# A two-layer graph convolution on one core: rows sent by kind, tile 1 decoded like later tiles, VectorE's constants in its waits, other counts of idle products, and the last position turned

## The chip, the cores and the metric

The kernel runs on one core of a Trainium2 chip. The metric is the device time of one execution in microseconds (us), the median of several runs. Engines are named TensorE (PE in the rows; PEld is its weight load), VectorE (DVE), ScalarE (ACT), GpSimd (POOL) and SyncE (SP). SPq, ACTq and POOLq are the DMA issues of an engine.

## The reference

There are 6250 nodes with 64 features and 200000 edges, sorted by destination. Cut to what matters:

```
deg_out = clip(segment_sum(1, src), 1);  deg_in = clip(segment_sum(1, dst), 1)
norm    = rsqrt(deg_out[src] * deg_in[dst])
conv(x, W1, W2):
    msg = (x[src] @ W1 + (x[src] * x[dst]) @ W2) * norm
    return x @ W1 + segment_sum(msg, dst)
h = relu(layernorm(x));  h = relu(conv(h, W1_1, W2_1));  h = conv(h, W1_2, W2_2)
out = x + h
```

With S = sum over a node's edges of x[src] / sqrt(deg_out), a layer is x @ W1 + (S @ W1 + (S * x) @ W2) / sqrt(deg_in). The kernel computes that form.

## The kernel before

Nodes are laid out in 49 blocks of 128 (node 128 b + 4 r + s sits in partition 32 s + r of block b). The kernel makes a dense count matrix of the edges and multiplies with it, in four stages.

**Opening.** SyncE loads dst (L395, L396), then the last entries of each row (`prev_i`, L398, behind a memset by GpSimd) and four weight matrices (L402). VectorE makes its constants (L609 to L620; the last ones, `mask`, `of_v` and `select`, are what the edge weights are computed with), casts the samples of dst, `last` and `prev` (L625 to L628), and chooses rows (`choose_rows`, L631, L632). TensorE multiplies the choice with the samples (the windows, L910: one product for tile 0, six for tiles 1 to 6). VectorE counts, per tile, where each row begins (`find_begin`, L640 to L645), and GpSimd fetches the edges of a row of that tile with indirect DMAs (`fetch`, L480: src and dst apart). There are seven tiles of seven blocks; `p_rows` is what becomes keys, `rows` (three kinds: place, place x q, place x q x q) what becomes weights. Tile 0 and tile 1 are decoded by VectorE (`decode_early`, L652 to L670; tile 1 after block 2), the later tiles by GpSimd in five steps beside the units (`decode`, L493, by `DECODE`) with VectorE's `weigh` (L672) between them. For tiles 0 and 1 TensorE turns `p_rows` (`turn`, L914) and ScalarE copies it to `keys` (`save_keys`, L1056); for the later ones SyncE writes eight DMAs to a table (`turn_keys`, L414) and issues one transposing DMA. The rows go to the `stack`: for tile 0, the first two blocks straight from `rows`, six DMAs, five by SyncE (L408) and one by ScalarE (L1093), all behind `rows_ready`; all others through a table (L409 to L413, L437 to L443). After tile 1's rows SyncE loads x (`load_x`). TensorE issues products that nobody reads (`keep_running`, L897: 36, 28 and 90 of them) where it would stand still.

**Units.** There are 98 units, two per block. Before the products of a unit (`products`, L938: 24 products of 98 columns into a `slab`), TensorE computes pairs of edge weights (`weigh_hots`, L923: 2 products of 392 columns per pair, three pairs for two units), ScalarE saves each pair (`save_weights`, L1069), and after the unit it packs the slab to `words` (`save_words`, L1080). VectorE makes the low one-hots of a block (`low_hots`, L683, a ring of three). `pairs_beside(u)` says which pairs TensorE and ScalarE do with unit u: they are four pairs ahead of what the unit reads from unit 0 on. VectorE's statistics of x lie beside blocks 9 to 27 (`STATS_BESIDE`, three per block), parts of `unpack` beside later ones.

**Turn to layer 0.** After unit 97 VectorE sums the degrees; ScalarE takes the root; VectorE scales h by pieces (`scaled_piece`), ScalarE applies relu to each piece (the high part, L1113), VectorE takes the low part (`low_piece`). TensorE multiplies positions 0, 1 and 2 together as the pieces come (L1017).

**Positions.** 98 positions, 49 per layer: 49 products of 128 or 129 columns each (L1039), the tile of counts stationary, the parts of h moving. For a position that is done, ScalarE and VectorE form S (`save_sums`, `sums`), GpSimd the product with h, TensorE turns the pair (`turn_pair`, L979, fp32), ScalarE saves it (`save_t`), TensorE multiplies it with the weights (`weigh`, L991) and VectorE adds it into g1 or `x_sb` (`finish`, L829). In layer 1 this is done inside the next position, behind product 26 (`EARLY`) and product 43 (`LATE`). In the last position TensorE sums three totals behind product 23 (L1045 to L1048), one of which is the check that no packed count is full (L886, L887). The end of the last position is then done alone (L1051, L1052), SyncE stores the result (L446 to L450, four DMAs for each of five stretches), and the flag decides whether the general path is run (it is not, here).

Queues: each engine takes its instructions in the order written. Nothing is planned at run time; semaphores hold each where it reads what another writes.

## Time and profile before

| | us |
|---|---|
| median of 3 runs | 507.52 (507.25 to 509.15) |
| the profiled execution | 506.1 |
| its span | 504.4 |
| TensorE busy | 484.3 |
| VectorE busy | 422.3 |
| ScalarE busy | 249.7 |
| GpSimd busy | 139.1 |
| opening, to the first weighing | 0 to 22.3 |
| units | 24.5 to 185.8 |
| turn to layer 0 | 185.8 to 199.4 |
| positions 3 to 97 | 199.4 to 497.7 |
| end | 497.7 to 504.4 |

The span begins and ends with the engines' first and last instruction; the time of an execution also holds what lies around it, 1.7 us here. Rows with an instruction begin with its start from the span's start, then its duration.

### The profile page before, as it was taken

How to read it: one execution, taken by the hardware profiler on the slowest of the kernel's cores; microseconds unless marked ns; L12 is line 12 of the kernel's file. 1: busy time of each engine (PE TensorE's matmuls, PEld its weight loads, DVE VectorE, ACT ScalarE, POOL GpSimd, SP SyncE). 2: the span in 40 equal slices, each digit the busy share in tenths (PEclk: the TensorE clock that was granted, in tenths of full speed). 3: DMA queues.
4: the chain of work that ended last, by engine and by line, in shares of the span. 5: the costliest groups of instructions: out<-in, count | busy, mean ns of one | idle time of the engine just before them, and what ended most of it. 6: DMA issues, size and time to landing. Idle time of an engine off the chain costs nothing.

```text
span 504.4 us, 19900 instructions
## 1 busy us (share of the span) xinstructions
PE 484.3 (96%) x8018; PEld 458.6 (91%) x8018; DVE 422.3 (84%) x1092; ACT 249.7 (50%) x706; POOL 139.1 (28%) x376
## 2 busy tenths in 40 slices
PE   5889999999999979999999999999999999999994
PEld 5768888888888869999999999999999999999993
DVE  6999999999999957877777777777988888888883
ACT  1299999999999964433333333332111111111110
POOL 3412434334346301433333333332111111111110
PEclk9999999999999998999999999999999999999998
DMA  3258313021202000000000000000000200010000
GB/s 69 79 102 97 66 28 83 23 73 33 58 15 54 3 1 3 4 1 3 3 3 2 4 3 3 4 1 3 4 3 2 45 3 1 3 44 1 14 18 18
DMA packets 24791, 12.32 MB, mean 24 GB/s; under 512 B 21024, under 2 KB 23376, under 8 KB 24701
## 3 DMA queue, kind: packets, MB, share of 16 engines
q1 hardware_dynamic: 23997, 9.04, 9.2%
q0 software_dynamic: 672, 2.01, 1.4%
q8 instruction: 64, 1.05, 0.9%
q14 instruction: 26, 0.21, 0.1%
q10 hardware_dynamic: 32, 0.01, 0.0%
HBM read 6.21 MB, written 4.05 MB: 20 GB/s over the span
## 4 chain that ended last, share of the span: by engine, by line
PE 88%; ACT 4%; DVE 4%; DMA 2%; issue 1%; SPq 0%; DVEq 0%; ACTq 0%
PE diff L1039 35%; PE slab L951 19%; PE iota_bank L1039 17%; PE diff L933 9%; ACT hots L1076 3%; PE diff L1010 2%; PE diff L1017 1%; PE slab L988 1%; DMA los<-in_dst_dram 1%; PE turn_t L988 1%; PE diff L1006 1%; ACT words L1084 1%; PE iota_bank L1017 1%; PE slab L1039 1%; DMA mixed<-rows 1%
## 5 line engine op out<-in xcount | busy, mean ns | idle before, releaser
L694 DVE TENSOR_TENSOR los<-mixed,iota_bank 128x5120 bf16<-128x5120 bf16 x49 | 137.5, 2809 | 5.2 <-PE slab L951 4.6
L951 PEld LDWEIGHTS slab<-hots,los 128*128 128x128 bf16 x2352 | 119.5, 98 | 13.6 <-ACT hots L1076 0.6
L951 PE MATMUL slab<-hots,los 128*128 128x98 fp8e5 x2352 | 125.4, 209 | 0.2 <-ACT hots L1076 0.2
L1076 ACT ACTIVATE hots<-diff 128x784 f16<-128x784 f32 x147 | 118.4, 848 | 6.3 <-PE diff L933 6.2
L1039 PE MATMUL diff<-late,mixed 128*128 128x128 f16 x1616 | 104.4, 219 | 0.0
L1039 PEld LDWEIGHTS diff<-late,mixed 128*128 128x128 fp8e4 x1616 | 98.7, 99 | 0.4
L1039 PE MATMUL diff<-los,mixed 128*128 128x129 f16 x1470 | 95.6, 220 | 0.0
L576 POOL TENSOR_TENSOR work<-work,h 128x64 f32<-128x64 f32 x98 | 31.5, 321 | 228.2 <-DVE work L811 228.2
L1039 PEld LDWEIGHTS diff<-los,mixed 128*128 128x128 fp8e4 x1470 | 89.3, 98 | 0.3
L933 PE MATMUL diff<-select,mixed 80*128 80x392 f16 x294 | 65.2, 329 | 3.2 <-ACT hots L1076 2.4
L740 DVE TENSOR_SCALAR mixed<-words 128x400 int32<-128x400 int32 x192 | 61.1, 358 | 0.0
L1084 ACT ACTIVATE words<-slab 128x441 uint16<-128x441 f32 x98 | 59.9, 611 | 2.2 <-PE slab L951 1.2
L1039 PE MATMUL iota_bank<-late,tile 128*128 128x128 f16 x784 | 51.5, 219 | 0.0
L1039 PE MATMUL iota_bank<-los,tile 128*128 128x129 f16 x735 | 49.0, 220 | 0.0
L1039 PEld LDWEIGHTS iota_bank<-late,tile 128*128 128x128 fp8e4 x784 | 48.0, 99 | 0.2
L1039 PEld LDWEIGHTS iota_bank<-los,tile 128*128 128x128 fp8e4 x735 | 45.0, 98 | 0.2
L487 POOL TENSOR_TENSOR hist<-hist,words 128x49 int32<-128x49 int32 x48 | 15.5, 324 | 104.9 <-ACT words L1084 81.1
L818 DVE SCALAR_TENSOR_TENSOR work<-h,stats,work 128x64 f32<-128x64 f32 x98 | 39.5, 403 | 4.5
L933 PEld LDWEIGHTS diff<-select,mixed 80*128 80x128 f16 x294 | 23.4, 98 | 12.2 <-ACT hots L1076 4.6
L740 DVE TENSOR_SCALAR tile<-words 128x400 int32<-128x400 int32 x96 | 30.6, 357 | 0.0
L1147 ACT ACTIVATE work<-diff,unscale 128x64 f32<-128x64 f32 x33 | 10.3, 313 | 38.1 <-PE diff L1039 37.1
L881 DVE TENSOR_TENSOR largest<-largest,words 128x900 uint16<-128x900 uint16 x47 | 29.0, 616 | 0.1
(177 smaller groups left out, 535.1 us busy)
## 6 DMA issues: line engine op xcount, KB each, us to landing
x_sb<-in_x_dram SPq DMA_DIRECT2D x4, 384.0 KB
rows_table<-rows SPq DMA_DIRECT2D x6, 252.0 KB, 2.5
mixed<-rows_table SPq DMA_DIRECT2D x18, 84.0 KB, 2.9
out_dram<-x_sb SPq DMA_DIRECT2D x8, 128.0 KB
los<-in_dst_dram SPq DMA_DIRECT2D x1, 750.0 KB
p_table<-p_rows_sb SPq DMA_DIRECT2D x20, 28.0 KB
p_table<-p_rows_sb SPq DMA_DIRECT2D x20, 7.0 KB
out_dram<-x_sb SPq DMA_DIRECT2D x4, 80.0 KB
```

The costliest lines, as they stand in the source:

```text
L487: nc.gpsimd.tensor_tensor(out=hist[:], in0=hist[:], in1=words[:, b, 0:Q - 1, WORDS // 2:WORDS // 2 + 2].bitcast(I32)[:, :, 0], op=ALU.add) ...
L576: nc.gpsimd.tensor_tensor(out=pair[a][:, 1], in0=s_sum[a], in1=h[:, b], op=ALU.mult).then_inc(product_ready, 1)
L694: nc.vector.tensor_tensor(out=los[:, b % LOS_RING].rearrange("e s (v t) -> e s v t", t=2), in0=key, in1=val, op=ALU.is_equal).then_inc(los ...
L740: ins = nc.vector.tensor_scalar(to, packed, 2 * s, 0x03030303, ALU.logical_shift_right, ALU.bitwise_and)
L818: nc.vector.scalar_tensor_tensor(pair[a][:, 0], h[:, b], root[:, b:b + 1], s_sum[a], ALU.mult, ALU.add).then_inc(pair_ready, 1)
L881: nc.vector.tensor_tensor(out=largest[:], in0=largest[:] if b > 1 else flat_words[:, 0:Q * SLOTS], in1=words[:, b].rearrange("p q s -> p ( ...
L933: ins = nc.tensor.matmul(diff[m % 2][:, bank, 0:HALF], stack[0:80, t % 2, j, k * 128:(k + 1) * 128], select[0:80, i * HALF:(i + 1) * HALF] ...
L951: ins = nc.tensor.matmul(to, los[:, u // 2 % LOS_RING, u % 2 * ULOWS + low], pairs, start=(step == 0), stop=(step == USTEPS - 1), skip_gro ...
L1039: ins = nc.tensor.matmul(bank(n)[:, 0:width], tiles[home(n)][:, q], parts[:, q, 0:width], start=(q == 0), stop=(q == BLOCKS - 1))
L1076: nc.scalar.activation(bass.AP(to.tensor, to.offset, [to.ap[0], [step, 2], [STEPS * BLOCKS, 8], [1, BLOCKS]]), diff[m % 2][:, :, 0:HALF].r ...
L1084: nc.scalar.activation(words[:, u // 2, 0:Q - 1, 9 * (u % 2):9 * (u % 2) + 9], bass.AP(mine.tensor, mine.offset + first, [mine.ap[0], [1, ...
L1147: nc.scalar.activation(s_hi[a], bank(n)[:, 0:D], ACT.Copy, scale=unscale).then_inc(hi_saved, 1)
```

## The change

- **Rows by kind.** Tile 0's rows are decoded in the same order, but each kind counts a semaphore of its own (`early_rows_ready` 1 and 2, then `rows_ready`). For the first two blocks SyncE sends kind 0 of both after the first, ScalarE kind 1 of both after the second, and after the third each sends one DMA of kind 2.
- **Tile 1 like later tiles.** GpSimd decodes it (steps 0 to 2 before unit 0, steps 3 and 4 at units 1 and 2), VectorE's `weigh(1)` stands after block 2, and its keys take SyncE's eight DMAs and the transposing DMA; TensorE's second `turn` and ScalarE's second `save_keys` go. x is loaded behind all that, and its statistics lie beside blocks 11 to 30.
- **Constants in waits.** VectorE's `mask` to `select` move between the begin of tile 0 and the windows of the others. The offset and the cast of prev come before the wait for dst. ScalarE casts the samples and issues the DMA of `prev_i`, of which GpSimd sets only row 0. The weights' DMAs wait for dst. Tiles 1 to 5 are counted with one comparison and one reduction.
- **Order of pairs.** TensorE and ScalarE have two pairs ahead at units 0 and 1, three at 2 and 3, four from unit 4 on.
- **Idle products.** 24, 28 and 76 in the opening; 34 more after unit 97 and 12 more ahead of the third round of pieces.
- **VectorE's own first pieces.** It applies relu to the first piece itself and takes the low parts of the first two pieces before it scales the third.
- **Last position turned.** Its 49 products have the parts stationary and the tile moving, so that S comes out turned, twice (S on partitions 0 to 63 and again, as high and low part, on 64 to 127). h of the last block is turned in position 95 and its product with W1 (`own_ps`) is added to `x_sb` in position 96. VectorE then scales S, and multiplies it with h turned; two fp32 products with weights stored twice give the rest. The sum of totals moves behind product 45. Two of the last four stores are issued by ScalarE.

```
```diff
+    DECODE.update({1: (1, 3), 2: (1, 4)})
+    WEIGH_BESIDE = {2: 1, **{u0 // 2 + 5: t for t, u0 in BEGIN.items()}}
...
-    STATS_BESIDE = [b for b in range(9, 34) if b not in WEIGH_BESIDE][:17]
+    STATS_BESIDE = [b for b in range(11, 34) if b not in WEIGH_BESIDE][:17]
...
+    def made(u):
+
+        return min(pairs_of(u) + 2 + min(u // 2, 2), UNITS * STEPS // 2)
+
     def pairs_beside(u):
 
-        first = 3 * (u // 2) + 4
-        return [m for m in ((first, first + 1) if u % 2 == 0 else (first + 2,)) if m < UNITS * STEPS // 2]
+        return range(made(u - 1) if u else 0, made(u))
...
-            sp.wait_ge(prev_set, 1)
-            sp.dma_start(prev_i[1:SROWS], bass.AP(dst.tensor, dst.offset + ROWLEN - GRAIN,
-                                                  [[ROWLEN, SROWS - 1], [1, GRAIN]])).then_inc(prev_in, 16)
+            sp.wait_ge(dst_in, 32)
...
             sp.wait_ge(stack_zeroed, 1)
+            sp.wait_ge(early_rows_ready, 1)
+            for j in range(2):
+                sp.dma_start(stack[0:16, 0, j], rows[16 * j:16 * j + 16, 0]).then_inc(first_in[j], 16)
             sp.wait_ge(rows_ready, 1)
-            for j in range(2):
-                for k in range(3):
-                    if (j, k) != (0, 1):
-                        sp.dma_start(stack[32 * k:32 * k + 16, 0, j], rows[16 * j:16 * j + 16, k]).then_inc(first_in[j], 16)
+            sp.dma_start(stack[64:80, 0, 0], rows[0:16, 2]).then_inc(first_in[0], 16)
...
+            def save_p(t):
                 sp.wait_ge(p_saved, t + 1)
-                if t > 2:
-                    sp.wait_ge(keys_in, 16 * (t - 2))
...
+            def turn_keys(t):
+                sp.wait_ge(p_out, 16 * 8 * t)
...
+            def save_rows(t):
+                sp.wait_ge(rows_ready, t + 1)
+                sp.wait_ge(stack_in, 48 * t)
+                sp.dma_start(rtab, rows[:]).then_inc(rows_out, 16)
+
             for t in range(1, TILES):
-                if t >= 2:
-                    turn_keys(t)
-                sp.wait_ge(rows_ready, t + 1)
+                save_p(t)
                 if t == 1:
-                    sp.wait_ge(rest_in, 48)
+                    save_rows(t)
...
             for b0, b1 in STORES:
                 sp.wait_ge(y_ready, b1)
-                for s in range(4):
+                for s in range(4 if b1 < BLOCKS else 2):
...
+            for step in range(3):
+                decode(1, step)
...
+            v(nc.vector.tensor_scalar(offset[:], group0[:], -1.0, 1.0, ALU.mult, ALU.add))
+            dve.wait_ge(prev_set, 1)
             dve.wait_ge(prev_in, 16)
             v(nc.vector.tensor_copy(prev[:], prev_i[:, GRAIN - 1:GRAIN]))
+            dve.wait_ge(dst_in, 32)
+            v(nc.vector.tensor_copy(last[:], dst_i[:, ROWLEN - 1:ROWLEN]))
...
+            def find_begins():
+                dve.wait_ge(window_ready, 2)
+                v(nc.vector.tensor_tensor(out=junk[:, 1:6], in0=windows[1][:, :, 0:SAMPLES],
+                                          in1=group0[:, 1:6].unsqueeze(2).to_broadcast([ROWS, 5, SAMPLES]), op=ALU.is_lt))
+                v(nc.vector.tensor_reduce(out=before[:, 1:6], in_=junk[:, 1:6], axis=AX.X, op=ALU.add))
+                count_before(6, windows[2][:, 0])
+                add_windows(1, 6, windows[1])
+                add_windows(6, TILES, windows[2])
+                bound_begin(1, TILES)
...
+                v(nc.vector.scalar_tensor_tensor(rows[:, 0].bitcast(U16), place, 8 * 2048.0, place, ALU.is_le, ALU.mult))
+                nc.vector.tensor_tensor(out=shared, in0=shared, in1=own, op=ALU.mult).then_inc(early_rows_ready, 1)
+                dve.wait_ge(early_rows_ready, 1)
+                nc.vector.scalar_tensor_tensor(rows[:, 1], q_i, -float(MID), rows[:, 0], ALU.add,
+                                               ALU.mult).then_inc(early_rows_ready, 1)
+                dve.wait_ge(early_rows_ready, 2)
+                nc.vector.scalar_tensor_tensor(rows[:, 2], q_i, -float(MID), rows[:, 1], ALU.add,
+                                               ALU.mult).then_inc(rows_ready, 1)
...
+            scaled_piece(1)
+            qs = slice(*PIECES[0])
+            dve.wait_ge(scaled_ready, 1)
+            nc.vector.tensor_scalar(parts0[:, qs, 0:D], scaled[:, qs], 0.0, None, ALU.max).then_inc(first_hi0_ready, 1)
+            low_piece(0)
+            low_piece(1)
+            scaled_piece(2)
+            for i in range(3, len(PIECES)):
...
+                    dve.wait_ge(own_ready, 1)
+                    v(nc.vector.tensor_tensor(out=x_sb[:, BLOCKS - 1], in0=x_sb[:, BLOCKS - 1], in1=own_ps, op=ALU.add))
                     dve.wait_ge(largest_taken, BLOCKS - 1)
-                    v(nc.vector.tensor_scalar(largest[:], largest[:], FULL, None, ALU.is_ge))
-                    nc.vector.tensor_reduce(out=totals[:, 2:3], in_=largest[:], axis=AX.X,
-                                            op=ALU.max).then_inc(totals_ready, 1)
+                    v(nc.vector.tensor_reduce(out=totals[:, 2:3], in_=largest[:], axis=AX.X, op=ALU.max))
+                    nc.vector.tensor_scalar(totals[:, 2:3], totals[:, 2:3], FULL, None, ALU.is_ge).then_inc(totals_ready, 1)
                 if n == POSITIONS - 1:
-                    dve.wait_ge(totals_summed, 1)
+                    dve.wait_ge(acc_ready, n + 1)
+                    nc.vector.tensor_scalar(s_t, bank(n)[:, 0:128], unscale1[:, 0:1], None,
+                                            ALU.mult).then_inc(last_ready, 1)
+                    dve.wait_ge(h_t_saved, 1)
+                    nc.vector.scalar_tensor_tensor(product_t, bank(n)[:, 0:128], unscale1[:, 0:1], h_t,
+                                                   ALU.mult, ALU.mult).then_inc(last_ready, 1)
+            dve.wait_ge(totals_summed, 1)
...
-            keep_running(36)
+            keep_running(24)
...
-            turn(0)
-            keep_running(90)
+            turn()
+            keep_running(76)
...
+            keep_running(34)
...
+                if i == 2:
+                    keep_running(12)
...
+                    if n == POSITIONS - 1:
+                        ins = nc.tensor.matmul(bank(n)[:, 0:128], parts1[:, q, 0:2 * D], tiles[home(n)][:, q],
+                                               start=(q == 0), stop=(q == BLOCKS - 1))
+                    else:
+                        ins = nc.tensor.matmul(bank(n)[:, 0:width], tiles[home(n)][:, q], parts[:, q, 0:width],
+                                               start=(q == 0), stop=(q == BLOCKS - 1))
+                    if n == POSITIONS - 3 and q == EARLY - 16:
+                        pe.wait_ge(z_used, BLOCKS)
+                        for half in range(2):
+                            turned_h = nc.tensor.matmul(h_turn_ps[half * D:(half + 1) * D], h[:, BLOCKS - 1], ident[:],
+                                                        start=True, stop=True)
+                        turned_h.then_inc(h_turned, 1)
+                    if n == POSITIONS - 2 and q == EARLY + 8:
+                        pe.wait_ge(h_t_saved, 1)
+                        nc.tensor.matmul(own_ps, h_t[0:D], wt[0:D, 1], start=True, stop=True).then_inc(own_ready, 1)
                     if q in turns:
                         turn_pair(turns[q])
                     if q in weighs:
                         weigh(weighs[q])
-                    if n == POSITIONS - 1 and q == EARLY - 3:
+                    if n == POSITIONS - 1 and q == LATE + 2:
...
-            turn_pair(POSITIONS - 1)
-            weigh(POSITIONS - 1)
+            n = POSITIONS - 1
+            pe.wait_ge(w_in, 128)
+            pe.wait_ge(y_ready, n - 1 - BLOCKS)
+            pe.wait_ge(last_ready, 1)
+            nc.tensor.matmul(turn_z[n % 2][:, 0:D], s_t, wt_twice[:, 0], start=True, stop=False)
+            pe.wait_ge(last_ready, 2)
+            nc.tensor.matmul(turn_z[n % 2][:, 0:D], product_t, wt_twice[:, 1], start=False, stop=True).then_inc(z_ready, 1)
...
+            act.wait_ge(dst_in, 32)
+            nc.scalar.activation(samples[:, 0:SAMPLES], dst_i[:, GRAIN - 1:ROWLEN:GRAIN], ACT.Copy).then_inc(samples_ready, 1)
+            save_keys()
...
+            act.wait_ge(early_rows_ready, 2)
+            for j in range(2):
+                act.dma_start(stack[32:48, 0, j], rows[16 * j:16 * j + 16, 1]).then_inc(first_in[j], 16)
             act.wait_ge(rows_ready, 1)
-            act.dma_start(stack[32:48, 0, 0], rows[0:16, 1]).then_inc(first_in[0], 16)
-            for m in range(4):
-                save_weights(m)
+            act.dma_start(stack[64:80, 0, 1], rows[16:32, 2]).then_inc(first_in[1], 16)
...
+                if n == POSITIONS - 2:
+                    act.wait_ge(h_turned, 1)
+                    nc.scalar.activation(h_t, h_turn_ps, ACT.Copy).then_inc(h_t_saved, 1)
...
+            act.wait_ge(y_ready, BLOCKS)
+            for s in range(2, 4):
+                part, n = node_rows(out, s, BLOCKS - 1, BLOCKS)
+                act.dma_start(part, x_sb[32 * s:32 * s + n, BLOCKS - 1:BLOCKS]).then_inc(y_out, 16)
```

## Rows read from the trace of the kernel before

**Rows 1.** The page: busy time of TensorE; the chain, by engine.
```profile
PE 484.3 (96%) x8018; PEld 458.6 (91%) x8018; DVE 422.3 (84%) x1092; ACT 249.7 (50%) x706; POOL 139.1 (28%) x376
...
PE 88%; ACT 4%; DVE 4%; DMA 2%; issue 1%; SPq 0%; DVEq 0%; ACTq 0%
```

**Rows 2.** Timeline of TensorE to 40 us: start, duration, instruction, idle before.
```profile
3.37 4.02 PE L900 MATMUL diff<-identb 128*128 128x128 bf16 x36 [3.37 <-POOL identb L474]
...
16.37 5.19 PE L900 MATMUL diff<-identb 128*128 128x128 bf16 x90
22.31 0.82 PE L933 MATMUL diff<-select,mixed 80*128 80x392 f16 x4 [0.76 <-DMA mixed<-rows]
...
37.10 0.51 PE L933 MATMUL diff<-select,mixed 80*128 80x392 f16 x2 [0.64 <-ACT hots L1076]
```

**Rows 3.** Timeline of VectorE to 40 us.
```profile
7.29 0.24 DVE L625 CAST los<-los 125x100 f32<-125x100 int32 x1 [0.23 <-DMA los<-in_dst_dram]
...
9.81 0.16 DVE L650 TENSOR_SCALAR offset<-group 112x7 f32<-112x7 f32 x1
...
12.55 0.32 DVE L640 TENSOR_SCALAR_CACHE_REDUCE los<-diff,group 112x100 bf16<-112x100 f32 x1 [1.83 <-PE diff L910]
...
15.21 0.35 DVE L658 TENSOR_SCALAR work<-late 112x384 int32<-112x384 int32 x1
```

**Rows 4.** Timeline of GpSimd to 40 us.
```profile
11.69 1.17 POOL L480 DMA_INDIRECT late<-in_src_dram,begin_i  x1 [7.52 <-DVE begin_i L645]
...
16.81 1.26 POOL L480 DMA_INDIRECT late<-in_dst_dram,begin_i  x1 [0.31 <-issue]
```

**Rows 5.** All instructions of line 408: durations in ns, first and last start.
```profile
L408 SPq DMA_DIRECT2D mixed<-rows x5: 589/589/606, 18.9 to 21.4; - x5
...
DMA to landing us min/median/max: 1.8/2.0/2.6
```

**Rows 6.** Timeline of ScalarE to 40 us.
```profile
26.12 2.28 ACT L1076 ACTIVATE hots<-diff 128x784 f16<-128x784 f32 x3 [1.00 <-PE diff L933]
...
34.69 0.62 ACT L1060 ACTIVATE mixed<-turn_t 128x224 bf16<-128x224 f32 x2
```

**Rows 7.** Timeline of SyncE's queue, 36 to 72 us.
```profile
35.67 6.88 SPq L393 DMA_DIRECT2D x_sb<-in_x_dram  x5
50.68 0.98 SPq L421 DMA_DIRECT2D p_table<-p_rows_sb  x1
...
63.83 1.26 SPq L442 DMA_DIRECT2D mixed<-rows_table  x3
```

**Rows 8.** Windows of 1 us: five engines' busy time, granted clock, DMA.
```profile
191.00:192.00 1.00, 1.00 (x13) 1.00 (x11) 1.00 (x3) 0.51 (x2) 0.00 (x0) 0.50 0.00 0
```

**Rows 9.** Timeline of TensorE, 176 to 216 us.
```profile
188.44 0.51 PE L1017 MATMUL diff<-los,late 128*128 128x129 f16 x6 [2.64 <-DVE los L790]
...
190.29 1.70 PE L1017 MATMUL diff<-los,late 128*128 128x129 f16 x14 [0.26 <-DVE los L790]
...
194.11 0.98 PE L1017 MATMUL diff<-los,late 128*128 128x129 f16 x14
...
199.41 1.39 PE L1039 MATMUL slab<-los,mixed 128*128 128x129 f16 x21
```

**Rows 10.** Timeline of VectorE, 474 to 505 us.
```profile
494.50 1.09 DVE L887 TENSOR_REDUCE totals<-largest 128x1 f32<-128x900 uint16 x1
...
500.20 0.28 DVE L839 SCALAR_TENSOR_TENSOR x_sb<-diff,stats,x_sb 128x64 f32<-128x64 f32 x1 [0.69 <-PE diff L1010]
```

**Rows 11.** Timeline of TensorE, 474 to 505 us.
```profile
495.64 0.19 PE L1047 MATMUL slab<-totals,ones 128*1 128x3 f32 x2 [1.32 <-DVE totals L887]
...
497.03 0.39 PE L1010 MATMUL diff<-wt,work 128*128 128x64 f32 x2
497.25 0.45 PE L1039 MATMUL diff<-late,mixed 128*128 128x128 f16 x5
```

**Rows 12.** Line 450 (stores) from 497 us, durations in ns.
```profile
L450 SPq DMA_DIRECT2D out_dram<-x_sb x8: 293/343/446, 497.8 to 501.6; - x8
```

198 lines of the change are left out of this document (95 added, 103 removed).

## The prediction

> **What bounds the kernel now.** I read the page first: busy shares and the chain by engine [rows 1]. The reader is to see that TensorE is busy 96% of the span and holds 88% of the chain. Every other engine matters only where TensorE waits. So I next looked for TensorE's idle time in the timeline, and found it in three places: the opening, up to unit 6 [rows 2 to 7]; the turn from the histogram to layer 0 [rows 8, 9]; and the last position [rows 10 to 12]. Between them it never stands for as much as half a microsecond at a time, and the change moves only VectorE's statistics there, two blocks later. The sum below is therefore three local sums, made against the profiled execution: 506.1 us, of which 504.4 is span.
>
> **Opening, up to the first weighing.** Before, the first weighing starts at 22.31 and is released by a DMA of rows [rows 2]. Backwards from there:
> - VectorE's casts of samples and prev (pitches of 0.15 and 0.19) go from between dst's landing and the choice of rows: the first to ScalarE (cast beside `last` and `later`, 0.5 us of cover), the second in front of the wait. The offset (0.20) goes ahead too. So begin 0 is found 0.54 earlier, and that is what the first fetch waits for.
> - In the wait for the windows (1.83 idle [rows 3]) VectorE now builds `mask` to `select`, 5.00 to 7.06 before, 2.1 us. It then comes to the windows at 12.3, and TensorE has them at about 12.2: no loss, no cover left.
> - Five counts of 0.37 pitch become one comparison of 500 elements and one reduction. No row shows them. Nearest is a reduction of 900 elements in 1.09 us [rows 10]: by its share 0.6 for each of the two, 1.2 for both, between 0.9 and 1.8. Begin 1 to 6 is then found at 14.6 and not at 15.3.
> - Decoding tile 0 starts at 15.21 before, behind those counts [rows 3]. It now starts when the counts end or the first fetch lands, if that is later. The fetch is issued at 11.69 before [rows 4], 0.54 earlier after, and landed in at most 3.5 us: by 14.7. I take 0.6 earlier; bounds 0.2 and 0.8.
> - SyncE issues its five row DMAs one behind another from 18.9, 0.59 to 0.61 each [rows 5]; the second, begun at 19.5, holds up unit 0. Now kinds 0 and 1 go while kinds 1 and 2 are still computed (0.6 each), half of them by ScalarE, idle then. At `rows_ready` only one issue is left ahead of unit 0. That is worth one issue, 0.6, plus up to 0.3 of spread in landing (1.8 to 2.6 [rows 5]).
> Together 1.4 us earlier, weighing at 20.9; bounds 0.6 and 1.9. The dst DMA no longer shares the engines with the weights' four DMAs; I count 0 to 0.3 for it, inside the bounds. Prev's DMA goes ahead of ScalarE's table load (1.28), whose result is wanted only at 16.6; the smaller memset and the merged semaphores cost and bring nothing, since their engines wait there.
>
> The selection work now lies beside GpSimd's first fetch. The first fetch takes 1.17 us beside an idle VectorE and one beside its decoding 1.26 [rows 4], so at most 0.3 is lost. [...]
>
> **Idle products.** 36 become 24, 90 become 76. The spacing tells the clock: 36 in 4.02 us is 112 ns each, 90 in 5.19 is 58 [rows 2]; the granted column says 1.00 throughout this stretch and is of no use here. So the 1.2 GHz level holds until after the second batch (28), the 2.4 GHz level from 16.4. With 76 x 58 ns from 15.7 the third batch ends at 20.1, before 20.9. If the clock rises 2 us later it ends at 21.1 and costs 0.2.
>
> **Units 0 to 6.** Tile 1 loses TensorE's turn (0.15) and ScalarE's four copies, 1.05 us from 34.69 to 35.74. TensorE's wait of 0.64 at 37.10 is for a weight save queued behind them [rows 2, 6]. That is 0.8. The new order puts unit 1 at two pairs less, so it begins over 1 us earlier. Unit 4 has its pairs as late as before, since ScalarE must by then have saved as many. I take 0.7; bounds 0.15 (the turn alone) and 1.7 (ScalarE's 1.00 idle ahead of 26.12 as well). VectorE gives back 2 us (four of decode_early's seven operations go), so it is not the next bound. It has 5.2 us of idle over all 49 blocks.
>
> **What is queued behind.** SyncE now carries tile 1's keys: 8 issues of 0.85, the transposition 2.23, and only then x [rows 7]. From 26.9 that is 38.8 for x and 47.3 for its last issue, where before it ended at 42.6. First, keys of tile 1 are wanted by VectorE at 41.3 (block 7) and land at 39.3. Second, x is wanted from block 11, 58 us. Third, tile 2's save is free to start at 47.9. Its rows are issued at 63.83 and land at 66.9, where the weighing for unit 28 starts at 68.0: 1 us of slack, and x ends just before. I count none of it and keep 1 us for the range. GpSimd's decoding of tile 1 (0.51, 0.51, 0.58) fits from 18.5 to 21.2, five microseconds before VectorE's `weigh`.
>
> **The turn to layer 0.** TensorE is idle 2.64 us before the first piece at 188.44. The granted clock is 0.50 from 190.4 to 193.7, and 14 products take 1.70 us where 14 later take 0.98 [rows 8, 9]. The 34 idle products (2.0 us at 58 ns) fill the wait, end at 187.7, and delay nothing; 12 more fill the wait for piece 2 (0.7 us). With the high clock: 18 products of the third round from 190.35, then five rounds of 21 and one of 7, all at 58 ns, so 190.35 + 1.05 + 5 x 1.22 + 0.41 = 197.9. VectorE's pieces arrive each 1.07 and stay ahead. Before it is 199.41: 1.5 us. VectorE's own first pieces make piece 1 ready 0.5 earlier, which lands in the wait for piece 2 (ready 0.1 later). Bounds: 0 if the clock falls all the same, 1.9.
>
> **The tail.** Added: in positions 95 and 96 three fp32 products, of 128, 128 and 64 columns. An fp32 product of 64 columns holds TensorE 0.22 (two instructions from 497.03, the next product at 497.25 [rows 11]), so 0.22, 0.22 and 0.22, up to 1.1 if 128 columns cost twice; 0.7. Removed:
> - TensorE's wait of 1.32 for the totals (reduction 494.50 to 495.59 [rows 10, 11]). Its product moves behind product 45, which runs at 496.4 with the 0.7 above; the totals come at 496.3, as VectorE shifts too. The whole wait goes, 1.45 with the restart behind it; the slack is 0.1.
> - From the last product's end to the last `x_sb`: 497.70, ScalarE 497.74, VectorE 498.14 and 498.46, TensorE 498.96, ScalarE 499.32, TensorE 499.65, VectorE 500.20 [rows 10], 2.5 us. After: two VectorE operations on 128 columns (0.3, 0.35), one fp32 product (0.44) and three hand-overs, 1.3; VectorE comes 0.1 late from position 96's own sum.
> The last `x_sb`: 0.7 - 1.45 - 1.1, or 1.9 earlier. Then two stores of four go to ScalarE: they are issued from 500.5 to 501.9 at 0.34 each [rows 12], so 0.6. The maximum is taken before the comparison (0.15 on one column for 0.38 on 900), which pays for the sum of own products (0.2). The second copy of the weights is loaded before layer 0, with DMA idle. The flag's four small operations (0.7) now stand behind the last `x_sb`, under the stores' landing. Tail: 2.5; bounds 1.2 and 3.5.
>
> **Sum.** 1.4 + 0.7 + 1.5 + 2.5 = 6.1 us off 506.1, which is 500.0 for a profiled execution. The median of the runs lies 1.4 above the profiled one, 507.5, so **501.4**.
>
> **Rivals.**
> 1. As summed: 72%.
> 2. TensorE's clock falls at the turn to layer 0 after all, or begin and rows gain little because a fetch or a landing takes the place: 1.5 or 1.0 of the sum is gone, in the worst case both, so 503 to 504. For it: even now the clock falls 2 us after TensorE has resumed, so what precedes decides. Against it: the wait is filled. 15%.
> 3. A queue takes over: keys of tile 1 or rows of tile 2 come late behind x on SyncE. Each stalls TensorE once, 1 to 3 us, so 502.5 to 504.5. For it: 1 us of slack. Against it: the save starts at its old distance to TensorE. 8%.
> 4. Slower than before: the clock at the opening. TensorE does 26 idle products less, and stands 2.2 us ahead of the first window, where it stood 1.2. If its clock were still low in the third batch, 76 x 112 ns would end at 24.2, 3.3 late, and each microsecond of units at 1.2 GHz costs half of itself. To lose all 6.1, it must stay low until about 30. Rising at 33, 509. For it: 64 products and 7 windows had not raised it before. Against it: the last batch follows without more idle than now. 3%.
> 5. An edit does not do what it says, as where the last position's weights (fp16, changed per product) cannot hide their load: 49 x 50 ns, 2.4 us, so 503.8. Unit products with 16-bit weights come each 47 ns (24 in 1.12 us), which speaks against it. 2%.
>
> A measurement of this kernel tells 0.5%, 2.5 us, from no change, so faster means below 505.0. Case 1 is faster, and most of 2, 3 and 5; about 9 in 100 of all lose enough to stay within it, and case 4 is the slower side: faster 0.88, same 0.09, slower 0.03. The range for 8 in 10 goes from 499.3 (sum 8.2) to 505.0 (2.5), taking in most of cases 2 and 3. All lower bounds together would be 2.0 and all upper ones 9.0, neither of them likely.
>
> **What would show it.** First weighing at 20.9 and unit 6 at 35.3; x's last issue before 48; no granted clock of 0.50 around 190; layer 0's fourth position 3.6 earlier than 199.4; no TensorE wait in the last position; 1.3 us from its last product to the last `x_sb`. The sum is wrong if the third batch of idle products is spaced 112 ns, or if units wait for a DMA near 45 or 66.

## The result and the profile after

The changed kernel takes 504.0 us (median of 4 runs, 503.6 to 505.4) beside 508.0 for the kernel before, measured with it: a ratio of 0.9926 (95% interval 0.9904 to 0.9948), 4.0 us faster. In two later groups of runs the same two kernels gave 501.8 for 506.2 (0.9925, 0.9895 to 0.9954) and 501.5 for 505.6 (0.9909, 0.9885 to 0.9932). So the gain is 4.0 to 4.4 us where 6.1 were forecast. The first profile after is of the 505.4 us run, the slowest of its four; its span is 503.6.

The page after, busy times and chain [rows 1]: TensorE's share of the chain is now 91% (88 before), and ScalarE's and VectorE's have halved, from 4% to 2% each.
```profile
PE 485.2 (96%) x8042; PEld 457.8 (91%) x8042; DVE 422.7 (84%) x1081; ACT 248.5 (49%) x701; POOL 142.1 (28%) x380
...
PE 91%; DVE 2%; DMA 2%; ACT 2%; issue 1%; SPq 0%; POOL 0%; DVEq 0%; ACTq 0%; POOLq 0%
```
TensorE's timeline in the opening, after [rows 2]. The third batch of idle products is spaced 58 ns (76 in 4.41), and the first weighing starts at 20.86, as forecast. But unit 0 (24 products from 23.35) takes 2.13 us, where 24 took 1.29 before: the granted clock falls to 0.50 at 23.4, for 3.4 us. This is called the low clock below (1.2 GHz; 1.00 is 2.4).
```profile
15.43 4.41 PE L955 MATMUL diff<-identb 128*128 128x128 bf16 x76
20.86 0.82 PE L986 MATMUL diff<-select,mixed 80*128 80x392 f16 x4 [1.02 <-DMA mixed<-rows]
...
23.35 2.13 PE L1004 MATMUL slab<-hots,los 128*128 128x98 fp8e5 x24
25.28 0.85 PE L986 MATMUL diff<-select,mixed 80*128 80x392 f16 x2
25.92 1.69 PE L1004 MATMUL slab<-hots,los 128*128 128x98 fp8e5 x24
```
VectorE after [rows 3]: the unshown pair, one comparison and one reduction, took 0.66 and 0.67 (forecast 0.6 each), and decoding starts at 14.27, 0.94 earlier.
```profile
12.03 0.66 DVE L672 TENSOR_TENSOR los<-diff,group 112x500 bf16<-112x500 f32 x1
12.73 0.67 DVE L674 TENSOR_REDUCE before<-los 112x5 f32<-112x500 bf16 x1
...
14.27 0.35 DVE L688 TENSOR_SCALAR work<-late 112x384 int32<-112x384 int32 x1
```
GpSimd after [rows 4]. The fetch beside `select` took 1.17 us again, as beside an idle VectorE, so that overlap cost nothing. The last row is one to keep in mind: tile 2's sources are now fetched at 22.06.
```profile
11.10 1.17 POOL L502 DMA_INDIRECT late<-in_src_dram,begin_i  x1 [6.93 <-DVE begin_i L661]
...
22.06 1.00 POOL L502 DMA_INDIRECT late<-in_src_dram,begin_i  x1 [0.28 <-issue]
```
SyncE's queue after, around x [rows 7]: tile 1's keys are turned at 35.53, x goes from 38.38 to 47.3, tile 2's rows at 63.17. No unit waited for a DMA, so rival 3 did not come.
```profile
35.53 1.24 SPq L439 DMA_TRANSPOSE mixed<-p_table  x1
37.01 1.32 SPq L460 DMA_DIRECT2D mixed<-rows_table  x3
38.38 8.88 SPq L405 DMA_DIRECT2D x_sb<-in_x_dram  x8
...
63.17 1.27 SPq L460 DMA_DIRECT2D mixed<-rows_table  x3
```
The turn to layer 0 after, TensorE [rows 9]. The 14 products at 190.80 are those of the first two rounds, those at 192.85 begin the third. They take 0.98 where they took 1.70: there is no low clock.
```profile
187.79 2.06 PE L955 MATMUL diff<-identb 128*128 128x128 bf16 x34
190.80 0.97 PE L1064 MATMUL diff<-los,late 128*128 128x129 f16 x14 [0.95 <-DVE los L831]
...
192.85 0.98 PE L1064 MATMUL diff<-los,late 128*128 128x129 f16 x14 [0.23 <-DVE los L831]
...
200.44 1.39 PE L1090 MATMUL slab<-los,mixed 128*128 128x129 f16 x21
```
The tail after, VectorE and TensorE [rows 10, 11]: no wait for the totals, last product ends at 498.54, last `x_sb` starts at 499.74.
```profile
498.58 0.35 DVE L940 TENSOR_SCALAR mixed<-diff,unscale 128x128 f32<-128x128 f32 x1 [0.22 <-PE diff L1087]
498.85 0.34 DVE L943 SCALAR_TENSOR_TENSOR mixed<-diff,unscale,mixed 128x128 f32<-128x128 f32 x1
499.74 0.28 DVE L887 SCALAR_TENSOR_TENSOR x_sb<-diff,stats,x_sb 128x64 f32<-128x64 f32 x1 [0.56 <-PE diff L1117]
```
```profile
488.60 0.44 PE L1095 MATMUL slab<-ident,h 128*64 128x128 f32 x4
...
498.07 0.19 PE L1107 MATMUL slab<-totals,ones 128*1 128x3 f32 x2
498.20 0.34 PE L1087 MATMUL diff<-mixed,late 128*128 128x128 fp8e4 x3
499.07 0.41 PE L1115 MATMUL diff<-mixed 128*128 128x64 f32 x2 [0.53 <-DVE mixed L940]
```
The stores: SyncE [rows 12] and ScalarE. The last is issued 1.0 us earlier than before, but the program ends only 0.8 earlier.
```profile
L472 SPq DMA_DIRECT2D out_dram<-x_sb x6: 313/400/446, 498.4 to 500.6; - x6
```

### The profile page after: what moved, and what is told of

Its sections match the earlier page's. It is cut to its first block, busy times and chain, and to the rows that moved or that the text cites. A ratio compares the mean times of both kernels' runs of the same rounds, so it can differ in the third digit from the quotient of the medians.

```text
span 503.6 us, 19945 instructions
## 1 busy us (share of the span) xinstructions
PE 485.2 (96%) x8042; PEld 457.8 (91%) x8042; DVE 422.7 (84%) x1081; ACT 248.5 (49%) x701; POOL 142.1 (28%) x380
## 4 chain that ended last, share of the span: by engine, by line
PE 91%; DVE 2%; DMA 2%; ACT 2%; issue 1%; SPq 0%; POOL 0%; DVEq 0%; ACTq 0%; POOLq 0%
PE diff L1090 34%; PE slab L1004 21%; PE iota_bank L1090 17%; PE diff L986 10%; PE diff L1055 2%; ACT hots L1141 1%; PE turn_t L1033 1%; DMA los<-in_dst_dram 1%; PE diff L1051 1%; PE slab L1033 1%; PE diff L1064 1%; PE slab L1090 1%; PE diff L1087 1%; DMA late<-in_dst_dram,begin_i 1%; PE iota_bank L1064 1%
## 5 line engine op out<-in xcount | busy, mean ns | idle before, releaser
L1004 PEld LDWEIGHTS slab<-hots,los 128*128 128x128 bf16 x2352 | 120.8, 98 | 13.3 <-issue 0.3
L1004 PE MATMUL slab<-hots,los 128*128 128x98 fp8e5 x2352 | 126.6, 209 | 0.0
L1090 PE MATMUL diff<-late,mixed 128*128 128x128 f16 x1567 | 101.3, 219 | 0.0
L1090 PEld LDWEIGHTS diff<-late,mixed 128*128 128x128 fp8e4 x1567 | 95.8, 98 | 0.5
L1090 PE MATMUL diff<-los,mixed 128*128 128x129 f16 x1470 | 95.7, 220 | 0.0
L1090 PEld LDWEIGHTS diff<-los,mixed 128*128 128x128 fp8e4 x1470 | 89.3, 98 | 0.3
L986 PE MATMUL diff<-select,mixed 80*128 80x392 f16 x294 | 66.6, 330 | 5.0 <-ACT hots L1141 3.9
L1090 PE MATMUL iota_bank<-late,tile 128*128 128x128 f16 x784 | 51.7, 219 | 0.0
L1090 PE MATMUL iota_bank<-los,tile 128*128 128x129 f16 x735 | 49.0, 220 | 0.0
L1090 PEld LDWEIGHTS iota_bank<-late,tile 128*128 128x128 fp8e4 x784 | 48.0, 98 | 0.4 <-issue 0.2
L1090 PEld LDWEIGHTS iota_bank<-los,tile 128*128 128x128 fp8e4 x735 | 45.1, 98 | 0.2
L986 PEld LDWEIGHTS diff<-select,mixed 80*128 80x128 f16 x294 | 22.9, 98 | 15.6 <-ACT hots L1141 8.8
```

The costliest lines, as they stand in the source:

```text
L986: ins = nc.tensor.matmul(diff[m % 2][:, bank, 0:HALF], stack[0:80, t % 2, j, k * 128:(k + 1) * 128], select[0:80, i * HALF:(i + 1) * HALF] ...
L1004: ins = nc.tensor.matmul(to, los[:, u // 2 % LOS_RING, u % 2 * ULOWS + low], pairs, start=(step == 0), stop=(step == USTEPS - 1), skip_gro ...
L1090: ins = nc.tensor.matmul(bank(n)[:, 0:width], tiles[home(n)][:, q], parts[:, q, 0:width], start=(q == 0), stop=(q == BLOCKS - 1))
```

## One span cut into stages, for every kernel run

Since each profile is of one execution, and these differ by 5 us for one and the same kernel, I cut every span at the same marks of TensorE: the first weighing, unit 6, the last unit product, position 3, position 93. A mark is the start of the weight load, which lies up to 0.2 us ahead of the product itself. The columns add up to the span (us), but for rounding.

| profile of | 1st weighing | to unit 6 | to last unit product | to pos. 3 | to pos. 93 | to end | span |
|---|---|---|---|---|---|---|---|
| before, 1st | 22.3 | 15.0 | 148.3 | 13.8 | 280.9 | 24.1 | 504.4 |
| before_again | 22.3 | 15.3 | 150.5 | 12.8 | 280.9 | 24.1 | 506.0 |
| before_fetch_late | 21.6 | 15.7 | 148.7 | 13.8 | 280.9 | 24.1 | 504.8 |
| after, 1st | 20.8 | 16.6 | 150.3 | 12.7 | 280.9 | 22.3 | 503.6 |
| after_again | 20.9 | 14.6 | 147.5 | 12.7 | 280.9 | 22.4 | 498.9 |
| after_third | 20.4 | 16.1 | 147.5 | 12.7 | 280.9 | 22.4 | 500.0 |
| order_old | 20.7 | 16.2 | 147.5 | 12.7 | 280.9 | 22.4 | 500.4 |
| open_idle_old | 20.6 | 14.6 | 149.8 | 12.7 | 280.9 | 22.3 | 500.9 |
| rows_old | 20.6 | 14.8 | 149.9 | 12.7 | 280.9 | 22.5 | 501.3 |
| tile1_old | 22.1 | 16.5 | 150.3 | 12.7 | 281.1 | 22.0 | 504.7 |
| fetch2_first | 22.0 | 17.0 | 147.5 | 12.7 | 280.9 | 22.4 | 502.4 |
| no_mid_idle | 20.7 | 15.0 | 150.2 | 13.0 | 280.9 | 22.4 | 502.2 |
| tail_old | 20.5 | 14.6 | 147.5 | 12.7 | 280.9 | 24.4 | 500.5 |
| mended | 20.3 | 14.6 | 148.7 | 12.5 | 280.9 | 22.0 | 499.0 |

## The experiments

Three chips; each group shares its runs of the kernel before, so times are compared inside a group and ratios between groups.

**Group 1 (before: 506.2).**

*after_again*: no edit.


> The changed kernel once more, unaltered. Its first profile gained what the sum said at four places (first weighing at 20.86 us, turn to layer 0 shorter by 1.1, tail shorter by 2.15) but lost 1.25 us of it in units 0 and 1, which ran with a granted clock of 0.50 (1.2 GHz), and about 2 us more in units 12 to 94, in steps of 0.4 to 0.5 us during which no engine raised a semaphore. Theory C (chance): these two losses belong to that one execution, which was also the slowest of the four (505.44 against 503.6 to 504.3); here unit 6 starts near 35.5 to 36.5 instead of 37.60, unit 94 near 181 instead of 183.30, span about 502, ratio to before 0.990 to 0.992. Theory S (structure of the new kernel: fewer idle products ahead of the units, a denser queue on SyncE): units 0 and 1 show 0.50 again, unit 94 starts after 182.5, span 503 to 504, ratio 0.993.


501.79 us. Theory C: both losses of the first profile are gone (14.6 and 147.5 in the table), and the first product of unit 6 starts at 35.6 (35.3 was forecast). The windows that tell it, after and after_again, from 24 to 26 us (columns: busy time of TensorE, its weight loads, VectorE, ScalarE, GpSimd; granted clock; DMA): 21 instructions at 0.50 in one, 41 at 1.00 in the other.
```profile
24.00:26.00 2.00, 2.00 (x21) 1.65 (x20) 2.00 (x1) 0.88 (x2) 0.00 (x0) 0.50 0.26 82
```
```profile
24.00:26.00 2.00, 2.00 (x41) 1.86 (x39) 2.00 (x1) 1.72 (x3) 0.00 (x0) 1.00 0.33 89
```

*order_old*:
```diff
-        return range(made(u - 1) if u else 0, made(u))
+        first = 3 * (u // 2) + 4
+        return [m for m in ((first, first + 1) if u % 2 == 0 else (first + 2,)) if m < UNITS * STEPS // 2]
...
+            for m in range(3):
+                weigh_hots(m)
...
+                if u == 0:
+                    weigh_hots(3)
```


> The changed kernel with the old order of weighings and products: three weighings, the products of unit 0, the fourth weighing, and then four ahead from the first unit on. My theory: the new order (unit 0 begins after four weighings, the lead grows by one per block) is worth a few tenths at the start and nothing later, so this kernel is slower than the changed one by 0 to 0.7 us (0.1%). Rival O (the new order opens the units with TensorE waiting between weighings, which is what drops the clock to 1.2 GHz in units 0 and 1): here units 0 and 1 run at 2.4 GHz, unit 6 starts near 35.5, and the kernel is 0.5 to 1.2 us faster than the changed one.


501.63 us against 501.79: no difference that this can measure. Rival O is out: the low clock came here too, for 6.8 us from 23.5. What the order is worth alone stays open; its profile has twice the low clock of after_third's, and yet takes about the same to unit 6 (16.2 and 16.1).

*tail_old*:
```diff
-                    if n == POSITIONS - 1:
-                        ins = nc.tensor.matmul(bank(n)[:, 0:128], parts1[:, q, 0:2 * D], tiles[home(n)][:, q],
...
-            nc.tensor.matmul(turn_z[n % 2][:, 0:D], s_t, wt_twice[:, 0], start=True, stop=False)
-            nc.tensor.matmul(turn_z[n % 2][:, 0:D], product_t, wt_twice[:, 1], start=False, stop=True).then_inc(z_ready, 1)
+            turn_pair(POSITIONS - 1)
+            weigh(POSITIONS - 1)
```


> The changed kernel with the old end: the last position is multiplied with the tile as the stationary side, its sums go through ScalarE, VectorE, GpSimd, a transpose and one product with the weights; no h turned ahead, no own part added ahead, flag reduced in the old order, TensorE waits for the totals three products before EARLY of the last position, four stores on SyncE. My theory: the stretch from position 95 to the end is 15.7 in the changed kernel and 17.9 here, so this kernel is 2.1 to 2.5 us slower than the changed one (0.4 to 0.5%). Rival: what the turned position gains (about 1.2 from the last product to the last x_sb, 1.45 of the totals wait) is eaten by its own products, and the difference is under 1 us.


503.20 us, 1.4 more than after_again; ratio to before 0.9941 (0.9921 to 0.9961), an interval that overlaps with after_again's, so the landmarks decide. Position 93 to the end is 24.4 here and 22.4 with the new tail: 2.0 us. TensorE's wait of 1.32 for the totals is back. The mechanism is as forecast, and its size just under the 2.1 to 2.5 expected.

*open_idle_old*:
```diff
-            keep_running(24)
+            keep_running(36)
...
-            keep_running(76)
+            keep_running(90)
```


> The changed kernel with 36 and 90 idle products in the opening instead of 24 and 76. My theory: the 14 extra ahead of the first weighing cost 14 x 58 ns = 0.8 us there (first weighing 21.7 instead of 20.9), the 12 extra at the start fall into a wait; the kernel is 0.5 to 0.8 us slower than the changed one if the clock is no different. Rival K (the shorter idle stretch is what lets the granted clock fall to 0.50 in units 0 and 1): with the old numbers units 0 and 1 run at 2.4 GHz, which gives back 1.25 us, so the kernel is 0.4 us faster or the same.


501.22 us, and the first weighing is at 20.7, not 21.7. My expectation was wrong: 14 more idle products cost nothing, since TensorE waited for rows anyway, and now ends them as these land. Units 0 and 1 run at 2.4 GHz, as rival K says; but so they do in after_again.

**Group 2 (before: 508.5).**

*before_again*: no edit.


> The kernel before, unaltered, for a second profile of it and for what two equal kernels differ by: ratio 1.000 within 0.003. My theory on the turn to layer 0: TensorE's wait there lets the granted clock fall to 0.50 in every execution, so it shows a stretch of 0.50 of about 3.4 us just behind the first pieces again, and the stretch from the end of the units to position 3 is again 13.8 us where the changed kernel has 12.7. From unit 6 to the end of the units I expect 147.5 us with stalls of 0 to 2 us on top, at other units than in the first profile (theory C, chance). Rival: the fall at the turn was the chance of one execution, and the stretch is 12.7 to 13.0 here.


508.13 us, ratio 1.0003 (0.9986 to 1.0019). From unit 6 on it takes 150.5: the kernel before has the same stalls here as the first profile after. The windows from 70 to 80 us of after, before_again and after_again: 161 instructions in the first two, 173 in the third, at a granted clock of 1.00 each time.
```profile
70.00:80.00 10.00, 9.64 (x161) 8.14 (x159) 9.93 (x11) 9.58 (x16) 4.59 (x7) 1.00 0.11 27
```
```profile
70.00:80.00 10.00, 9.64 (x161) 8.14 (x159) 9.93 (x13) 9.59 (x16) 4.30 (x7) 1.00 0.11 26
```
```profile
70.00:80.00 10.00, 10.00 (x173) 8.75 (x170) 9.96 (x13) 9.93 (x17) 4.79 (x7) 1.00 0.19 45
```
The low clock at the turn is there again, but here it begins at 190.5, before the first piece (191.0), and part of it falls ahead of the third round, where TensorE waits for VectorE anyway. The stretch is 12.8, not the 13.8 that I expected. So the low clock recurs, and what it costs depends on where it falls.

*no_mid_idle*:
```diff
-            keep_running(34)
...
-                if i == 2:
-                    keep_running(12)
```


> The changed kernel without the 34 and the 12 idle products at the turn to layer 0. My theory: the idle products alone hold the clock; without them 0.50 is granted for about 3.4 us behind the first pieces and the stretch from the end of the units to position 3 takes 13.8 us, not 12.7, so the kernel is 1.1 to 1.5 us slower than the changed one. Rival: VectorE's own first pieces are what shortened the stretch (they were late, not the clock); then the stretch stays at 12.7 to 13.0 and the time is the same within 0.3 us, or even shorter by 0.2, since the 34 idle products end close to the first pieces.


505.34 us, ratio 0.9950 (0.9930 to 0.9971), against 0.991 to 0.993 for the unaltered one; the intervals overlap. The low clock is back (window below). It is in all four profiles without these idle products and in none of the ten with them, which shows that they hold the clock. The stretch is 13.0 where it is 12.7 with them, 0.3 us in this execution, since the low clock began at 188.4, ahead of the first piece again.
```profile
190.00:191.00 1.00, 0.99 (x10) 0.73 (x7) 0.89 (x3) 1.00 (x3) 0.00 (x0) 0.50 0.05 11
```

*rows_old*:
```diff
-            sp.wait_ge(early_rows_ready, 1)
             for j in range(2):
-                sp.dma_start(stack[0:16, 0, j], rows[16 * j:16 * j + 16, 0]).then_inc(first_in[j], 16)
-            sp.wait_ge(rows_ready, 1)
-            sp.dma_start(stack[64:80, 0, 0], rows[0:16, 2]).then_inc(first_in[0], 16)
+                for k in range(3):
+                    if (j, k) != (0, 1):
+                        sp.dma_start(stack[32 * k:32 * k + 16, 0, j], rows[16 * j:16 * j + 16, k]).then_inc(first_in[j], 16)
...
-            act.wait_ge(early_rows_ready, 2)
```


> The changed kernel with tile 0's row DMAs sent as before, all behind the last kind: five on SyncE and one on ScalarE. With 14 more idle products the first weighing was no later, so the idle products don't set it. My theory: the DMAs of rows do, and one issue ahead of unit 0 was worth 0.6: the first weighing is at 21.4 to 21.8 here instead of 20.5 to 20.9, unit 6 0.5 to 0.9 later, and the kernel 0.6 us slower. Rival F: the earlier begin and decoding on VectorE did it all (begin 0 found 0.5 earlier, decoding 0.9), the way the rows are sent is worth under 0.2: first weighing under 21.1.


503.65 us, ratio 0.9923 (0.9896 to 0.9951), as the unaltered one's. First weighing at 20.6. Rival F: sending the rows by kind was worth nothing. SyncE issues all five behind the last kind and they land in 1.8 us. In the three profiles of the changed kernel SyncE's second early issue took 0.88 to 1.43 us instead of 0.6, and its two early DMAs took 2.2 to 2.7 us to land. So the last DMA that the first weighing needs left SyncE at 18.5 to 19.0, and here at 18.7: the early issues won no time for the late one.
```profile
L418 SPq DMA_DIRECT2D mixed<-rows x5: 589/589/607, 18.1 to 20.6; - x5
...
DMA to landing us min/median/max: 1.7/1.8/1.8
```
```profile
L416 SPq DMA_DIRECT2D mixed<-rows x2: 601/1016/1432, 16.9 to 17.5; - x2
...
DMA to landing us min/median/max: 2.2/2.5/2.7
```

*tile1_old*:
```diff
-    DECODE.update({1: (1, 3), 2: (1, 4)})
-            for step in range(3):
-                decode(1, step)
...
+                if b == 2:
+                    decode_second()
...
+                if u == 3:
+                    turn(1)
...
+                if u == 4:
+                    save_keys(1)
```


> The changed kernel with tile 1 as before: decoded by VectorE behind block 2, its keys turned by TensorE behind unit 3 and spread by ScalarE behind unit 4, no keys of tile 1 on SyncE. My theory: units 4 to 6 lose what the change won there, so unit 6 starts 0.4 to 0.8 us later than in the undisturbed profile of the changed kernel (35.41), the pitch of units 4 to 6 is near 4.1 again instead of 3.25, and the kernel is 0.4 to 0.8 us slower. Rival Q (the queue): eight more table DMAs and a transposition on SyncE in the units bring the stalls of 0.4 to 0.8 us, which are then rarer here, and the kernel is the same or faster than the changed one.


505.78 us, ratio 0.9939 (0.9916 to 0.9961). By the median it is slower (the interval overlaps with the unaltered one's), but not mainly where I said: the pair of units 4 and 5 takes 3.68 (4.06 before, 3.24 after_again), the stalls are there as well (150.3, so rival Q is out), and 1.2 to 1.7 us are lost ahead of the first weighing (22.1 against 20.4 to 20.9 in the three unaltered profiles), which the edit was not meant to touch. GpSimd's timeline shows what moved: with nothing of tile 1 to decode, it fetches tile 2's sources at once.
```profile
18.74 0.95 POOL L499 DMA_INDIRECT late<-in_src_dram,begin_i  x1 [0.15 <-issue]
```

**Group 3 (before: 505.6).**

*fetch2_first*:
```diff
+            fetch(2, 0)
             for step in range(3):
                 decode(1, step)
```


> The changed kernel with one call moved: GpSimd fetches tile 2's sources before it decodes tile 1, as the kernel before does by having nothing to decode there, and not behind it. Theory G: the gain at the first weighing beyond VectorE's earlier decoding is this fetch, which in the changed kernel is issued at 21.6 to 22.3 instead of 19.3 (18.7 in the kernel with tile 1 as before, whose first weighing was at 22.05 although its rows were sent as early as in the changed kernel); its packets no longer stand among those of tile 0's rows. Then the first weighing here is at 21.7 to 22.1 instead of 20.6 to 20.9, and the kernel is 1 us slower than the changed one. Rival: something else of tile 1 (ScalarE, SyncE) made it late there; then the first weighing stays at 20.5 to 20.9.


502.52 us, 1.0 more than after_third's 501.53, but the ratios 0.9929 (0.9904 to 0.9954) and 0.9909 (0.9885 to 0.9932) overlap, so the landmarks decide. The first weighing is at 21.98 with a wait of 1.96 for rows: theory G. The DMA of rows that SyncE issues at 18.9, behind the fetch, lands after 2.9 us; the same one took 1.7 in the first profile after and 1.8 in after_third. GpSimd's fetch, TensorE's first weighing and that DMA here:
```profile
18.55 0.95 POOL L502 DMA_INDIRECT late<-in_src_dram,begin_i  x1 [0.16 <-issue]
```
```profile
21.98 0.82 PE L987 MATMUL diff<-select,mixed 80*128 80x392 f16 x4 [1.96 <-DMA mixed<-rows]
```
```profile
L418 SPq DMA_DIRECT2D mixed<-rows x1: 589/589/589, 18.9 to 18.9; - x1
...
DMA to landing us min/median/max: 2.9/2.9/2.9
```
From the start of VectorE's last kind of rows to that weighing it is 4.5 us here, 4.1 in both profiles of the kernel before and 4.4 in tile1_old, which all fetch early; it is 2.9 to 3.5 in the three profiles of the changed kernel. The Trainium skill (DMA: Bandwidth & Descriptors, "Issuing engines are not separate DMA queues") has it that DMAs started by SyncE, ScalarE and GpSimd run on the same 16 engines and interleave. By that a fetch ahead of the rows can delay them, and a second issuing engine saves issue time alone. The traces of fetch2_first (landing after 2.9 us instead of 1.7) and rows_old (first weighing at 20.6, as with two engines) agree.

*before_fetch_late*:
```diff
+    FETCH_AFTER = {1 if u == 0 else u: what for u, what in FETCH_AFTER.items()}
```


> The kernel before with one number changed: the fetch of tile 2's sources is issued in the turn of unit 1 instead of unit 0, so behind tile 0's rows. Theory G: the first weighing comes at 21.3 to 21.5 instead of 22.3, and the kernel gains 0.8 to 1.0 us (0.2%) over the kernel before by this alone; the rest of the opening's 1.4 is VectorE's (0.5 to 0.8). Rival: the first weighing stays at 22.1 to 22.3.


505.33 us, ratio 0.9988 (0.9967 to 1.0008): not told from no change. The profile shows the step: the first weighing starts at 21.61, 0.7 earlier, and without any wait, straight behind the 90 idle products, which are what holds it now. The 0.7 is gone by unit 1, which starts at 28.16 (28.08 in the kernel before), behind a wait of 1.01 for ScalarE. So moving the fetch alone won the kernel before nothing that can be measured.
```profile
18.79 2.96 PE L901 MATMUL diff<-identb 128*128 128x128 bf16 x50
21.61 0.82 PE L934 MATMUL diff<-select,mixed 80*128 80x392 f16 x4
...
27.83 0.49 PE L934 MATMUL diff<-select,mixed 80*128 80x392 f16 x2 [1.01 <-ACT hots L1077]
```

*mended*:
```diff
-            nc.vector.tensor_scalar(parts0[:, qs, 0:D], scaled[:, qs], 0.0, None, ALU.max).then_inc(first_hi0_ready, 1)
...
-                if i > 0:
...
-                        for half in range(2):
-                            turned_h = nc.tensor.matmul(h_turn_ps[half * D:(half + 1) * D], h[:, BLOCKS - 1], ident[:],
-                                                        start=True, stop=True)
+                        nc.tensor.matmul(h_turn_ps[0:D], h[:, BLOCKS - 1], ident[:], start=True,
+                                         stop=True).then_inc(h_turned, 1)
...
+                    nc.scalar.activation(h_t[0:D], h_turn_ps[0:D], ACT.Copy)
+                    nc.scalar.activation(h_t[D:2 * D], h_turn_ps[0:D], ACT.Copy).then_inc(h_t_saved, 1)
```


> The changed kernel with three edits. ScalarE makes the first piece again: VectorE doing it cost 0.34 us of VectorE ahead of the wait that counts, since the third round of products started 5.15 us behind the last unit in the changed kernel and 4.75 in the kernel before; I expect 4.75 to 4.8 again and position 3 0.35 earlier. The last block's h is turned by one product instead of two, and ScalarE copies it twice: position 95 0.2 to 0.25 us shorter. 36 and 84 idle products in the opening instead of 24 and 76: no cost, since rows land behind them. Together 0.5 to 0.6 us (0.1%) faster than the changed kernel, too little for the medians, so the landmarks of the profiles decide. Rival: ScalarE's first piece comes later than VectorE's did (0.42 and a hand-over for 0.34), so the turn is no shorter.


The two numbers of idle products are 36 and 84. 500.56 us, ratio 0.9893 (0.9869 to 0.9917), the fastest of all; 1.0 us less than after_third, with intervals that overlap. The first piece starts 2.87 us behind the last unit product, as in the kernel before (3.07 in the changed one), so VectorE's own first piece was a loss of 0.2. The stretch to position 3 gains that 0.2 only: the third round, expected 4.75 to 4.8 behind the last unit product, starts 4.95 behind it (5.11 in the changed kernel), since it now stands behind the 12 idle products, which end as it starts. Turning h once instead of twice won nothing: position 95 takes 3.60 us in both. The tail is still 0.4 shorter than in after_third, and 0.3 of it is in position 93, which the edits don't touch (see the tail in the next section).
```profile
187.89 0.83 PE L945 MATMUL diff<-identb 128*128 128x128 bf16 x12
188.55 0.97 PE L1054 MATMUL diff<-los,late 128*128 128x129 f16 x14
```

*after_third*: no edit.


> The changed kernel again, unaltered, on the chip of the other three, for the direct comparison and a third profile. I expect the landmarks of the second profile: first weighing 20.6 to 20.9, from the end of the units to position 3 12.7, from position 95 to the end 15.8; from unit 6 to the end of the units 147.5 or about 150, in whichever of the two states this chip shows also the kernel before (148.3 in its first profile, 150.5 in its second).


501.53 us. The stages are those of after_again, but for a first weighing 0.5 earlier and the clock: 0.50 from 23.0 for 3.4 us, in units 0 and 1, and 16.1 to unit 6 instead of 14.6. So one unaltered kernel has it in two of its three profiles, and in this one it costs 1.5 us.

## Why the prediction was right or wrong

The direction held, and all four places gained; but three of them gained less than forecast, and the total was 1.7 to 2.1 us too large. Compared with the kernel before's first profile, the undisturbed profile of the changed one (after_again) is 5.5 us shorter: 1.4 in the opening, 0.4 to unit 6, 0.8 in the units, 1.1 at the turn, 1.8 in the tail.

- **Opening, 1.4 (forecast 1.4): the sum came out by luck.** Its composition was wrong. Decoding earlier on VectorE was worth 0.6 to 0.8 (its last kind of rows starts at 17.4 to 17.6 instead of 18.2). The 0.6 that I gave to sending rows by kind was worth nothing (rows_old). The other 0.7 or more came from a step that the prediction took to be free: that GpSimd's decoding "fits from 18.5 to 21.2". It does, and it pushes tile 2's fetch, the next item in GpSimd's program, from 19.3 to 22 us and out of the rows' way (fetch2_first, before_fetch_late). I had looked at the queues behind SyncE, not behind GpSimd. These are the runs' figures at the first weighing; how much of the fetch's share reaches the end is not shown, since in the kernel before it was lost by unit 1.
- **Idle products in the opening.** The third batch ran at 58 ns and delayed nothing, as forecast. But TensorE then stands 0.4 to 1.0 us for rows. Rival 4 (a low clock at the opening) came in a small form, in units 0 and 1: 1.5 and 2.0 us in two of three profiles of the unaltered kernel. Of the nine profiles with 24 and 76 idle products five have it; the two with 36 and 84 or 90, and the three of the kernel before and its variant, have none. That the dropped idle products cause it is likely and not shown. There is a second sign. In four of those five the second batch of 28 had taken 2.1 to 2.4 us, not the 3.2 of the kernel before's first profile; TensorE's spacing had shortened within it, and TensorE then stood 1.1 to 1.4 us ahead of the turn. Three of the four without the low clock had 2.9 to 3.2, and 0.3 to 0.6 there. So "the 1.2 GHz level holds until after the second batch" was true of one profile, and not of all (2.12 in before_again).
- **Units 0 to 6, 0.7.** 0.4 where the clock stays high, against the first profile of the kernel before (0.7 against its second); with it low, a loss of 1.1 to 1.6. The gain from tile 1's work was as forecast: units 4 and 5 take 3.24, not 4.06. "Unit 4 has its pairs as late as before" was a little too good: it starts 11.4 behind the first weighing, where it was 11.1 and 11.3. ScalarE now saves three pairs in a row (2.27 us) ahead of units 2 and 4. The 2.3 us that the first profile loses behind unit 6 were no part of the change: the kernel before shows the same stalls (before_again).
- **The turn, 1.5.** Gained 1.1, 1.1 and 0.1 against the three profiles of the kernel before and its variant. "The clock falls": yes, in each of these three, and never with the idle products. From the third round's start to position 3 it is 9.1 us in two of the three, 8.0 in before_again and 7.6 with the idle products. So the low clock costs 1.5 in two profiles, as forecast, and 0.45 in the third, where it began 0.5 us before the first piece and part of it fell on the stretch in which VectorE sets the pace. The other part is a step that failed: "ready 0.1 later" for piece 2, the price of VectorE's own first pieces. The third round starts 5.1 behind the last unit product, not 4.7 to 4.8, so 0.3 to 0.4 is lost ahead of it. Piece 1 was to be ready 0.5 earlier; the second round starts 0.2 earlier, and the first 0.2 later, behind VectorE's extra 0.34.
- **The tail, 2.5.** 1.8 in each profile. The totals wait went, and from the last product's end to the last `x_sb` it is 1.2 (forecast 1.3). Counted from position 93, the last `x_sb` comes 1.5 earlier where I had 1.9: the three added fp32 products cost 0.9 and not 0.7 (positions 95 and 96 take 3.6 each, 3.1 before; position 95 takes this with two of them and, in mended, with one, so the second was free and the two places cost 0.47 each). And position 93 takes 3.42 where it took 3.13, also in tail_old, so this is no cost of the new products. TensorE waits there for VectorE, which starts its part of S 0.45 us behind ScalarE's in place of 0.09. In mended and tile1_old position 93 takes 3.13, so it isn't in the nature of the change; why VectorE starts late is open. The stores gave 0.5 of issue time, of which 0.2 went again: from the last issue to the end it is 3.0 and not 2.8. VectorE in after_again, then in mended:
```profile
477.50 0.28 DVE L859 SCALAR_TENSOR_TENSOR work<-iota_bank,unscale,work 128x64 f32<-128x64 f32 x1 [0.76 <-ACT work L1216]
```
```profile
477.60 0.28 DVE L849 SCALAR_TENSOR_TENSOR work<-iota_bank,unscale,work 128x64 f32<-128x64 f32 x1 [0.40 <-ACT work L1203]
```

The typical gain is then 1.4 + 0.4 + 0.8 + 1.8 = 4.4 us with a high clock in the units (0.8 being the mean over the three falls at the turn), less what the low clock takes in some executions: 1.5 in five of nine profiles, or 0.8 in the mean. That makes 3.6, somewhat under the measured 4.0 to 4.4.

## What to carry to other kernels

When an engine gets new work ahead of its loop, list what stood next in that engine's program: here a DMA issue moved by 3 us, and that was half of the gain at the first weighing. Forecast a cost or gain of the clock as a range and not as its full size: the same fall cost 1.5 us in two profiles and 0.45 in one, where it lay partly beside another engine's pace. And take a second profile of both kernels before explaining a microsecond: the first profile after seemed to blame the change for stalls that the kernel before has too.
